# First loads in order of use on two queues, and set-up work placed behind the first scores, in an AdaLN, attention and MoE kernel

## The reference, cut to what matters

```python
c = einsum('bsi,bij->bsj', x, cond_weight[ids]) + cond_bias[ids][:, None, :]   # ids: 16 categories
def lora_linear(x, W, b, A, Bm): return x @ W.T + b + x @ A.T @ Bm.T * (1.0 / 8)
Q, K, V = [lora_linear(c, W, b, A, Bm).reshape(64, 64, 16, 16) for each of q, k, v]
scores = einsum('bqhd,bkhd->bhqk', Q, K) / 4 + slopes * (pos_k - pos_q)
out = einsum('bhqk,bkhd->bqhd', softmax(scores), V).reshape(64, 64, 256)
x = x + c + rezero * lora_linear(out, Wo, bo, Ao, Bo)
z = (x @ lora_A[lang].T) @ lora_B[lang].T + lang_embed[lang]     # 4 languages, rank 16
logits = (z @ Wr + br) / 1.5                                     # 12 experts, the best 2 are used
x = x + geglu(z @ Ws1 + bs1) @ Ws2 + bs2 + sum over 2 experts of w_e * (geglu(z @ We1[e] + be1[e]) @ We2[e] + be2[e])
```

## Time and profile before

| | us |
|---|---|
| median of 3 executions | 856.76 (856.32 to 856.85) |
| profiled execution, whole | 856.82 |
| span of its trace | 854.9 |
| PE busy in the span | 824.7 (96%) |
| PE's share of the chain that ended last | 87% |

### The profile page before, as it was taken

How to read it: one execution, slowest core, us unless ns; L and a number is a source line. 1 busy time by engine, 2 the same in 40 slices (tenths; PEclk the granted TensorE clock), 3 DMA queues, 4 the chain that set the end, 5 groups by cost and what they waited for, 6 DMA issues and landing times.

```text
span 854.9 us, 28470 instructions
## 1 busy us (share of the span) xinstructions
PE 824.7 (96%) x9821; PEld 687.6 (80%) x9822; DVE 536.1 (63%) x1231; ACT 290.4 (34%) x783; POOL 405.6 (47%) x511
## 2 busy tenths in 40 slices
PE   7899999999999999889999999999999999999995
PEld 6778888888888888767777888888888888888884
DVE  3676666666666667757886566566666665665662
ACT  0233333333333333343333233333333333333330
POOL 2143344333334444200003367776776777777762
PEclk9999999999999999999999999999999999999998
DMA  9445555555555534014952323232232232222222
GB/s 283 142 113 168 169 169 169 169 169 158 155 157 164 160 113 106 16 38 158 269 214 63 106 34 41 32 37 34 31 38 33 32 39 31 33 38 32 36 31 26
DMA packets 49005, 85.61 MB, mean 100 GB/s; under 512 B 7266, under 2 KB 27554, under 8 KB 48834
## 3 DMA queue, kind: packets, MB, share of 16 engines
q1 hardware_dynamic: 33634, 68.76, 25.9%
q0 software_dynamic: 13888, 15.13, 13.2%
q10 hardware_dynamic: 1440, 1.16, 0.5%
HBM read 68.48 MB, written 16.55 MB: 99 GB/s over the span
## 4 chain that ended last, share of the span: by engine, by line
PE 87%; DVE 7%; ACT 2%; issue 1%; DMA 1%; ACTq 1%; POOL 0%; DVEq 0%
PE ps L1425 23%; PE ps L1411 13%; PE ps L1322 6%; PE ps L1123 4%; PE ps L1142 4%; PE ps L1406 4%; PE ps L1229 4%; PE ps L1170 4%; PE ps L1182 3%; PE ps L1110 3%; PE ps L1311 3%; PE ps L1233 2%; PE ps L1392 2%; DVE arena L732 2%; DVE arena L736 2%; ACT arena L542 2%
## 5 line engine op out<-in xcount | busy, mean ns | idle before, releaser
L1425 PE MATMUL ps<-arena,stage 128*128 x900 | 206.6, 379 | 0.0
L1425 PEld LDWEIGHTS ps<-arena,stage 128*128 128x128 f32 x900 | 165.2, 190 | 19.5
L478 POOL DMA_INDIRECT out_dram<-stage,to_row x75 | 120.6, 1608 | 86.8 <-DVE stage L1035 80.5
L634 ACT ACTIVATE stage<-ps 128x384 f32<-128x384 f32 x150 | 65.4, 488 | 240.3 <-PE ps L1411 240.3
L1411 PE MATMUL ps<-token_rows,token_rows_T 64*128 64x128 f32 x1800 | 141.5, 285 | 0.0
L1411 PEld LDWEIGHTS ps<-token_rows,token_rows_T 64*128 64x128 f32 x1800 | 118.0, 188 | 0.0
L470 POOL DMA_INDIRECT token_rows<-gated_rows,from_row x75 | 75.0, 1001 | 64.5 <-DVE to_row L920 41.9
L1011 DVE COPY token_rows<-ps 128x128 f32<-128x128 f32 x75 | 21.9, 292 | 126.4 <-PE ps L1393 126.4
L386 POOL TENSOR_TENSOR arena<-arena 128x256 f32<-128x256 f32 x32 | 23.3, 728 | 148.9 <-DVE arena L761 148.9
L1020 DVE TENSOR_TENSOR stage<-ps,stage 128x384 f32<-128x384 f32 x150 | 75.9, 548 | 1.8 <-ACT stage L634 1.8
L732 DVE TENSOR_REDUCE arena<-ps 128x16 f32<-128x1024 f32 x32 | 39.2, 1225 | 49.6 <-PE ps L1162 49.3
(11 more groups left out here) (170 smaller groups left out, 1483.9 us busy)
## 6 DMA issues: line engine op xcount, KB each, us to landing
stage<-in_we_dram SPq DMA_DIRECT2D x36, 512.0 KB, 4.1
arena<-in_cond_w_dram SPq DMA_DIRECT2D x64, 256.0 KB, 2.9
arena<-in_we_dram SPq DMA_DIRECT2D x12, 768.0 KB, 5.0
arena<-in_x_both_dram SPq DMA_DIRECT2D x32, 256.0 KB, 2.6
arena<-in_L_cond_bias_dram SPq DMA_DIRECT2D x64, 64.0 KB, 2.8
out_dram<-arena SPq DMA_DIRECT2D x32, 128.0 KB, 1.7
be_bc<-in_be_rows_dram SPq DMA_DIRECT2D x13, 192.0 KB, 2.8
gated_rows<-token_rows POOLq DMA_DIRECT2D x2, 1152.0 KB, 10.3
```

Source lines behind the costliest of these rows:

```text
L478: pool.indirect_dma_start(out_rows, bass.IndirectOffsetOnAxis(to_row[:, t:t + 1], 0), y_sb[t % YR], None, compute_op=ALU.add).then_inc(d_a ...
L634: nc.scalar.activation(g_sb[hf], ps[:, 2 + hf, 0:HH], ACT.Gelu).then_inc(g_ok, 1)
L1425: last = mm(ps[:, 4 + s % 2, 0:D], actT_sb[s % 2][:, hf, j * P:(j + 1) * P], arena[:, ds(e * E2 + (NJ * hf + j) * D, D)], start=(hf == 0 a ...
```

## The change

Transfers. ACT issues, behind `low`, only the first 132 columns of the constants (`consts` is reordered so that ident, kmask and kv stand first) and `small`, both counted by `d_first`; then bo and bv (`d_near`), the untransposed half of tile 0's x (`d_first_x`), and the rest (`d_rest`: the language map, the other columns of the constants, languages, lora A). SP issues only the transposed half of x first, then wT of k, both categories' register reads together, both `cond_w`, both biases, wT of q, the ALiBi table (counted by `d_near`), wT of v, tile 1's set, wT of o, bs2. `load_condition` has this order (both reads, both weights, both biases) in every tile. `PROJECTIONS` is now k, q, v, o.

Engines. DVE starts with the k weights, `c_add(0)`, the q weights, one small scaled bias, `k_spread(0)`, the v weights, then `ali`, `bo_rz` and the `vD` columns; the o weights, `tri_b`, the languages' one-hot and `lang_routers` come in tile 0 behind `k_spread(1)` (`lang_setup`), and the language rows behind `router_consts`. On PE `router_rows` moves into tile 0 ahead of `prob_transpose(0)`, `router_products` behind tile 0; eight more `warm` matmuls stand behind `condition(0)`; the wait for `ar_sb` moves from score(1) to the first merge. ACT copies the router rows in tile 0. POOL does the residuals of tiles 0 and 1, one after the other with their `residual_c`, ahead of the copy of the one-hot. The low-rank product for o goes to PSUM bank 7 and `warm` to bank 6.

The diff, cut to its core:

```diff
-CONST_COLS = dict(ident=P, tri=P, kmask=2, kv=2, count_down=NE, tile_start=NT, slot_tile=NS,
+CONST_COLS = dict(ident=P, kmask=2, kv=2, count_down=NE, tile_start=NT, slot_tile=NS, tri=P,
                   block=NLANG * NE, past_high=1, past_mid=1, lang_row=1, one_row=1,
                   in_tile=P, part_back=1, pad_row=1, id_high=2 * PAIRS, half=2)
+EARLY = P + 4
...
-        first_loads = [
-            (consts[:, :], a["consts"]), (small, a["small"]), (ali_f, a["alibi"]),
-            (aT.rearrange("p c l n -> p (c l n)"), a["lora_aT"]), (a_rows, a["lora_a"]), (ba[:, :, :].rearrange("p c n -> p (c n)"), a["lora_ba"]),
-            (lang_i[:, :], a["lang_of"]), (lang_b[:, :], a["lang_rows"]), (bv_half, a["bv_half"]), (bo_bc, a["bo_rows"])]
-        ALL_FIRST = 16 * len(first_loads)
-        PROJECTIONS = (1, 2, 0, 3)
+        near_loads = [(bo_bc, a["bo_rows"]), (bv_half, a["bv_half"])]
+        rest_loads = [
+            (ba[:, :, :].rearrange("p c n -> p (c n)"), a["lora_ba"]), (consts[:, EARLY:], a["consts"][:, EARLY:]),
+            (lang_i[:, :], a["lang_of"]), (lang_b[:, :], a["lang_rows"]),
+            (a_rows, a["lora_a"]), (aT.rearrange("p c l n -> p (c l n)"), a["lora_aT"])]
+        FIRST, NEAR, REST = 16 * 2, 16 * (len(near_loads) + 1), 16 * len(rest_loads)
+        PROJECTIONS = (1, 0, 2, 3)
...
-                for b in range(2):
-                    cat = sp.value_load(cat_i[0:1, ds(i * 2 + b, 1)], min_val=0, max_val=NCAT - 1)
+                cats = [sp.value_load(cat_i[0:1, ds(i * 2 + b, 1)], min_val=0, max_val=NCAT - 1) for b in range(2)]
+                for b, cat in enumerate(cats):
                     sp.dma_start(cond_w[s][:, b].rearrange("p c n -> p (c n)"), a["cond_w"][ds(cat, 1), :, :].rearrange(
                         "o p n -> (o p) n")).then_inc(d_cw[s], 16)
+                for b, cat in enumerate(cats):
                     sp.dma_start(cond_bias[s][b * S:(b + 1) * S, :], a["L0_cond_bias"][ds(cat, 1), :].rearrange(
                         "o n -> (o n)").partition_broadcast(S)).then_inc(d_cb[s], 16)
...
-            load_x(0, 0)
-            for n in PROJECTIONS[0:2]:
-                sp.dma_start(wm[n].rearrange("p c n -> p (c n)"), a["wT"][n]).then_inc(d_wT[n], 16)
+            sp.dma_start(x_in[0][:, D:2 * D], a["x_both"][0, :, D:2 * D]).then_inc(d_x[0], 16)
+            sp.dma_start(wm[PROJECTIONS[0]].rearrange("p c n -> p (c n)"), a["wT"][PROJECTIONS[0]]
+                         ).then_inc(d_wT[PROJECTIONS[0]], 16)
             sp.wait_ge(d_cat, 16)
             load_condition(0, 0)
-            for n in PROJECTIONS[2:]:
-                sp.dma_start(wm[n].rearrange("p c n -> p (c n)"), a["wT"][n]).then_inc(d_wT[n], 16)
+            n = PROJECTIONS[1]
+            sp.dma_start(wm[n].rearrange("p c n -> p (c n)"), a["wT"][n]).then_inc(d_wT[n], 16)
+            sp.dma_start(ali_f, a["alibi"]).then_inc(d_near, 16)
+            n = PROJECTIONS[2]
+            sp.dma_start(wm[n].rearrange("p c n -> p (c n)"), a["wT"][n]).then_inc(d_wT[n], 16)
+            load_tile(1, True)
+            n = PROJECTIONS[3]
+            sp.dma_start(wm[n].rearrange("p c n -> p (c n)"), a["wT"][n]).then_inc(d_wT[n], 16)
             sp.dma_start(bs2_bc[:, :], a["bs2_rows"]).then_inc(d_bs2, 16)
-            load_tile(1, True)
...
+            pool.wait_ge(s_first, 2)
+            residual(0, False)
+            residual_c(0, False)
+            residual(1, True)
+            residual_c(1, True)
             pool.wait_ge(s_hot, 1)
             nc.gpsimd.tensor_copy(lrows[:, :, NLR:NLR + NLANG], lang_hot).then_inc(s_row_rest, 1)
-            residual(0, False)
-            residual(1, True)
-            residual_c(0, False)
-            residual_c(1, True)
...
-            for dst, src in first_loads:
-                act.dma_start(dst, src).then_inc(d_first, 16)
+            act.dma_start(consts[:, 0:EARLY], a["consts"][:, 0:EARLY]).then_inc(d_first, 16)
+            act.dma_start(small, a["small"]).then_inc(d_first, 16)
+            for dst, src in near_loads:
+                act.dma_start(dst, src).then_inc(d_near, 16)
+            act.dma_start(x_in[0][:, 0:D], a["x_both"][0, :, 0:D]).then_inc(d_first_x, 16)
+            for dst, src in rest_loads:
+                act.dma_start(dst, src).then_inc(d_rest, 16)
...
-            dve.wait_ge(d_first, ALL_FIRST)
-            V.tensor_copy(ali, ali_f).then_inc(s_const, 1)
-            V.tensor_copy(tri_b[:, :], col["tri"]).then_inc(s_const, 1)
-            V.tensor_copy(lang_tmp, lang_b[:, :])
-            link(V.tensor_copy(lang_f, lang_i[:, :]))
-            link(V.tensor_scalar(lang_tmp, lang_tmp, col["lang_row"], col["one_row"], ALU.is_equal, ALU.add))
-            for hf in range(2):
-                V.tensor_scalar(langB[:, hf, :], lang_tmp, col["half"][:, hf:hf + 1], None, ALU.mult)
-            for lang in range(NLANG):
-                V.tensor_scalar(lang_hot[:, :, lang], lang_f, float(lang), None, ALU.is_equal)
-            dve.wait_ge(s_zero, 3)
-            for s in range(2):
-                for h in range(2):
-                    V.tensor_copy(vD[s][:, :, :, 32 + h],
-                                  col["kv"][:, h:h + 1].unsqueeze(2).to_broadcast([P, 2, 8]))
-            V.tensor_scalar(bq_quarter, bq_col, 0.25, None, ALU.mult)
-            V.tensor_scalar(bo_rz, bo_bc, rz, None, ALU.mult).then_inc(s_hot, 1)
-            dve.wait_ge(s_hot, 1)
-
...
+            def lang_setup():
+                low_rank_weight(3, PROJECTIONS[3])
+                dve.wait_ge(d_rest, REST)
+                V.tensor_copy(tri_b[:, :], col["tri"]).then_inc(s_const, 1)
+                V.tensor_copy(lang_tmp, lang_b[:, :])
+                link(V.tensor_copy(lang_f, lang_i[:, :]))
+                for lang in range(NLANG):
+                    ins = V.tensor_scalar(lang_hot[:, :, lang], lang_f, float(lang), None, ALU.is_equal)
+                ins.then_inc(s_hot, 1)
+                dve.wait_ge(s_hot, 1)
+                lang_routers()
+
+            def tile_steps(i, odd, between=lambda: None):
                 one_more, two_more = not isinstance(i, int) or i + 1 < NT, not isinstance(i, int) or i + 2 < NT
                 shift(i)
                 if one_more:
                     k_spread(i + 1)
+                between()
...
+            low_rank_weight(0, PROJECTIONS[0])
             c_add(0, False)
-            for at, n in enumerate(PROJECTIONS):
-                low_rank_weight(at, n)
-            lang_routers()
+            low_rank_weight(1, PROJECTIONS[1])
+            dve.wait_ge(d_first, FIRST)
+            V.tensor_scalar(bq_quarter, bq_col, 0.25, None, ALU.mult).then_inc(s_first, 1)
             k_spread(0)
+            low_rank_weight(2, PROJECTIONS[2])
+            dve.wait_ge(d_near, NEAR)
+            V.tensor_copy(ali, ali_f).then_inc(s_const, 1)
+            V.tensor_scalar(bo_rz, bo_bc, rz, None, ALU.mult).then_inc(s_first, 1)
+            dve.wait_ge(s_zero, 3)
+            for s in range(2):
+                for h in range(2):
+                    V.tensor_copy(vD[s][:, :, :, 32 + h],
+                                  col["kv"][:, h:h + 1].unsqueeze(2).to_broadcast([P, 2, 8]))
             v_spread(0, False)
             c_add(1, True)
-            tile_steps(0, False)
+            tile_steps(0, False, lang_setup)
             router_consts()
+            link(V.tensor_scalar(lang_tmp, lang_tmp, col["lang_row"], col["one_row"], ALU.is_equal, ALU.add))
+            for hf in range(2):
+                V.tensor_scalar(langB[:, hf, :], lang_tmp, col["half"][:, hf:hf + 1], None, ALU.mult)
...
+                if isinstance(n, int) and n == 0:
+                    pe.wait_ge(ar_sb, 1)
...
+                between()
                 if not isinstance(i, int) or i > 0:
                     output(i - 1)
                 prob_transpose(i)
...
             condition(0, False)
-            router_rows()
+            warm(8)
+            pe.wait_ge(d_first, FIRST)
             c_transpose(0)
             pe.wait_ge(s_mrgc, 1)
             project_k(0)
+            pe.wait_ge(s_mrgc, 2)
+            project_q(0)
             pe.wait_ge(s_mrgc, 3)
-            project_q(0)
             project_v(0)
             condition(1, True)
-            pe.wait_ge(s_mrgc, 4)
+            pe.wait_ge(s_const, 1)
+            tile_steps(0, False, 0, between=router_rows)
             pe.wait_ge(s_sp1c, 1)
             pe.wait_ge(s_zero, 4)
             router_products()
-            tile_steps(0, False, 0)
-            pe.wait_ge(ar_sb, 1)
+            pe.wait_ge(s_mrgc, 4)
             tile_steps(1, True, 0, merge_b=(0, 0, 16))
```

29 lines of the change are left out of this document (17 added, 12 removed).

## The result

The changed kernel takes **849.59 us** (median of four executions, 848.36 to 851.36), the kernel before took 856.81 on the same chip; the ratio is 0.9913, with an interval of 0.9899 to 0.9926. The two profiled executions, 856.82 and 850.41, differ by 6.4, their spans (854.9 and 848.4) by 6.5.

What follows compares the result with a forecast made beforehand. PE, busy 96% of the span, bounds the kernel; gains lie in its waits and slow clock at the start. 3.8 + 1.4 - 0.6 - 0.6 + 0.8 - 0.2 = 4.6 us off 856.82 gives 852.2, range 850.9 to 854.2.

Steps and rivals of the forecast that it cites:

- the gone wait of score(1): At tile 1's score on PE: it no longer waits for the router constants, a gain of 0.8 us.
- a wait for a transfer behind 11.5: Sign of being wrong: PE waits for a transfer later than 11.5 us.
- The first term: Start of tile 0 on PE: its transpose starts at 12.8 instead of 16.62, gaining 3.8 us (3.5 to 4.0).
- "Covered" for condition(1): Condition of tile 1, at 17.4: its second weight, issued at 10.9, lands by 16.5, so no wait.
- The clock, 1.4 us: Tile 0's projections on PE: the clock stays at 1.00, so 3.43 us become 2.05, gaining 1.4.
- DVE's order: Tile 0: PE waits for DVE's v weights, -0.6 us, and its attend for DVE's copy of the probabilities, -0.6 us.
- The constants ahead of the maximum of tile 1: DVE at tile 1: constants and language instructions between router products and the maximum cost 0.2 us (0 to 0.4).
- The engines' work is the same, so the lead is carried to the end: Behind tile 1: engines' work is unchanged and PE bounds itself, so the 4.6 us lead stays to the end.
- The clock did not fall: Rival, 9%: the clock falls all the same at the front, costing 1.4 us and up to 1 more; 853.6 to 854.6.
- the lead was not eaten: Rival, 6%: tile 2's set or the first merge's loads arrive as late as before, up to the whole gain; 856.
- `d_rest` was in time: Rival, slower, 3%: PE waits ahead of prob_transpose(0) for the six late loads; landed at 28.8 it gives 858.5.
- their rival's 852.5 to 853.5: Rival, 8%: transfers set the front, condition(0) or condition(1) waits up to 1.3 us; 852.5 to 853.5.

Runs made afterwards that it cites:

- e12: The changed kernel with the six rest loads issued by POOL once both condition weights of tile 0 have landed, no longer by ACT; ratio to the kernel before 0.9897.
- e2: The changed kernel without the eight added warm-ups behind condition(0); ratio to the kernel before 0.9927.
- e4: The kernel before with the change's transfers alone (new loads on both queues), its engines' order kept, no added warm-ups; ratio to the kernel before 0.9999.
- e5: The changed kernel with SP's and ACT's first loads in the order of before, so the engines' order alone; ratio to the kernel before 0.9937.
- e7: The changed kernel with only the o weights left behind k_spread(1), the rest of the language set-up behind v_spread(1); ratio to the kernel before 0.9906.
- e10: The changed kernel with the six rest loads issued by SP behind tile 1's set instead of by ACT; 853.63 us, ratio to the kernel before 0.9947.
- e14: The changed kernel with four warm-ups instead of eight behind condition(0); one run, 851.38 us.
- e9: The changed kernel with twelve warm-ups instead of eight behind condition(0); one run, 849.88 us.
- e1: The kernel before with eight more warm-ups behind condition(0); 857.61 us, ratio to the kernel before 0.9989.
- e3: The changed kernel with load_condition's old order (read, weight, bias, twice) from tile 2 on; ratio to the kernel before 0.9908.
- e6: The changed kernel with ACT's loads behind the early constants and small held until both condition weights of tile 0 are in; ratio to the kernel before 0.9922.
- e8: The changed kernel with its eight added warm-ups moved from behind condition(0) to the very first group; ratio to the kernel before 0.9903.
- e15: The changed kernel with sixteen warm-ups instead of eight behind condition(0); one run, 851.03 us.

## Why the prediction was wrong, point by point

**The direction and the places** were right: c_transpose(0), the clock, the two DVE waits, the gone wait of score(1), with no new bound behind tile 1. Of the prediction's own signs of being wrong one came true, a wait for a transfer behind 11.5 (condition(1), 16.98); and the distance behind tile 2 did change, but grew.

**The first term, 3.8 us up to c_transpose(0), was too small; it measured 4.8.** It failed as a chain of cautious terms. Both weights went out from 3.61 on, within 0.90 us, where I had 4.3 and 4.9 with 0.78 for each register read. The second landed by 8.96, some 4.8 us behind its issue, not 5.6. The landing time is no constant: the q weights, issued at 6.05, were there at 12.6. And the warm-up, which I took over with its 3.59 us, ended at 8.16. Fifteen of the seventeen traces have its 2.18, so the trace of before was one of the two slow ones, by chance. But the gain is not the 2.0 us by which the condition is early, because the next in line was never priced: the bias, issued at 5.52 and landed 5.66 us later. The prediction let DVE add it "meanwhile". e12, where it is in time, shows its price: the transpose is 1.25 us earlier.

**"Covered" for condition(1) was wrong by 0.6.** project_v to condition(1) is 1.48 us (16.98 - 15.50), before it was 0.92: tile 1's weights were late. It offset over half of the first miss.

**The clock, 1.4 us,** came as forecast: sixteen projections in 2.02 us against 3.43. It held although the transpose waited 1.24 us and condition(0) 0.79, where the prediction had no wait of over 0.6. As a term of the sum it was mis-read all the same: e2 loses it and is 0.2 us later at tile 1, since the waits behind it take up nearly all of it. Two terms that share a cover can't be added one by one.

**DVE's order:** the wait for the v weights was 0.67 (0.6), that of the attend 0.57 (0.6: 5.89 ahead at prob_transpose(0), 5.32 at the attend). The constants ahead of the maximum of tile 1 cost 0.2, as said. The ALiBi cast, bo_rz and the four copies took 1.5 us (15.36 to 16.85), not 0.9, against 1.14 for project_v (the 1.18 of the prediction is no row); PE did not wait for them.

**"The engines' work is the same, so the lead is carried to the end"** is the step that failed most, by 1.1 us. The work was the same, its time was not: with eight matmuls added ahead of the loop ten of its steps took some 0.1 us less each.

**The rest.** Between tile 31 and the end of the span lie 491.4 us before and 491.1 after, and in the other runs 490.0 to 493.4. The higher ones have a stretch with the granted clock at 0.50 near 360, the lower ones (e4, e5, e7, e10 to e14, up to 490.5) have not. e9 has none and takes 491.1; there PE stands 0.34 and 0.36 us for DVE, at 460 and at 472, where e7 has no such waits. The kernel before and the changed one had such a stretch in their traces. After's four executions lie 3.0 us apart, and their mean granted clocks go in the same order (0.993 at 851.36, 0.995 at 850.41, 0.996 at 848.76, 0.997 at 848.36), so such stretches are the likeliest reason, though not a shown one, why the median lies 0.8 below the profiled one. That is the last part of the 7.2. So: 4.6, + 1.0 - 0.6 at the front, + 1.1 in the loop, + 0.3 behind tile 31, and + 0.8 from profile to median, 7.2 in all.

**The rivals.** The clock did not fall, the lead was not eaten (e10 shows how it would have been), `d_rest` was in time. The transfers did bound the front, by the bias, by condition(0)'s 0.79 and by condition(1), but from an earlier start than I had, so that their rival's 852.5 to 853.5 did not come. The range left no room on the low side: its best end, 850.9, took every known term at its best and held nothing for a term that was not on the list. The loop's 1.1 us alone nearly make up the 1.3 by which the range was missed.

## What to carry over

When a wait at a start-up is removed, price every operand of the next step by its own issue and landing, the small ones too, and find which is last; a second queue helped here only where it took bytes and issues away from that one. A lead is kept only if the next set of loads moves up with it, so ask which engine's step releases them and what is issued ahead of them. A loop whose code is unchanged can still cost 0.1 us a pass more or less because of what was added ahead of it: read its step in both traces before a change of 1 us is put down to anything else.

## What the runs showed of the hardware

The same loop's step takes mostly 11.99, or 12.13 to 12.16 us, by the number of instructions ahead of it (one trace each of seventeen kernels). This was not expected.

The first matmuls have two paces under one reading of the clock: 36 of the same warm-ups took 3.59 us before, 3.44 in e14 and 2.18 in the other fifteen traces, and the column shows 1.00 in each, also in the stretch from 8 to 11 that the prediction leaned on the earlier trace rows. In these traces the column does not tell the pace ahead of its first change.

A wait of PE does not settle by its length alone whether the clock falls. Ahead of prob_transpose(31) PE waits 1.75 us in every trace, and the granted clock falls to 0.50 near 360 in eight of them (before, after, e1, e2, e3, e6, e8, e15) and in the other nine not. In the front it fell behind 1.79 us (e2) and not behind 1.51 (e8), each with no warm-ups between condition and transpose.

Four copies of 16 columns on DVE took 0.96 us beside POOL's addition (16.06 to 16.81), and 0.41 where POOL did nothing, as before and in e4:

```profile
16.30 0.41 DVE L702 COPY arena<-consts 128x16 f32<-128x16 f32 x4
```

The Trainium skill, "SBUF — State Buffer", has the port pair of the two engines locked for a whole instruction and the loser block. The trace agrees for DVE, which lost 0.55 us (0.97 in e12 as well); POOL's additions stayed at 0.73 to 0.75. The prediction had looked for the loss on POOL, and nobody waited for it on DVE.
